# Attention scores from two float32r parts, matmuls paired in two 64-row tiles, value matmuls half a stretch later

## What is computed

```python
# per sequence
h = _layernorm(x) * (1 + ca) + sa
q, k, v = lora_linear(h, wq, aq, bq), lora_linear(h, wk, ak, bk), lora_linear(h, wv, av, bv)   # 16 heads of 16
scores = jnp.einsum('bhqd,bhkd->bhqk', q, k) / jnp.sqrt(16.)
attn = jax.nn.softmax(jnp.where(causal, scores, -jnp.inf))
x = x + ga * lora_linear(jnp.einsum('bhqk,bhkd->bhqd', attn, v), wo, ao, bo)
h = _layernorm(x) * (1 + cb) + sb
x = x + gb * ffn(h)          # relu(h Wi^T + expert low rank), top 2 of 4 experts, then Wo
```

## Time and profile before

| what | value |
|---|---|
| three runs | 2151.85, 2151.95 and 2155.94 us, median 2151.95 us |
| span of the profiled execution (first to last instruction) | 2145.5 us |
| own time of the profiled execution | not on the page; the span is 6.4 us below the median of the runs |
| mean granted TensorE clock | 0.959 of full |
| TensorE matmul records, busy | 88% of the span |
| TensorE weight loads, busy | 46% |
| DVE, ACT, POOL busy | 56%, 44%, 25% |
| one turn of the loop | 251.1 us (its reload of the input at 320.0 and at 1575.4 us, five turns apart) |

### The profile page before, as it was taken

The page is one execution under the profiler, slowest core; times in us unless marked ns, Lnnn a source line. Parts: engine busy times, 40 slices in busy tenths (PEclk is TensorE's granted clock), DMA queues, the critical chain, the costliest instruction groups (busy, mean ns, idle before and its releaser), DMA issues.

```text
span 2145.5 us, 36829 instructions
## 1 busy us (share of the span) xinstructions
PE 1892.0 (88%) x11124; PEld 980.5 (46%) x11124; DVE 1199.8 (56%) x2697; ACT 938.8 (44%) x1701; POOL 529.7 (25%) x823
## 2 busy tenths in 40 slices
PE   8687888999889989899889998899898998798858
PEld 5233343455435454354534555354543545344435
DVE  3755567555665557655575556655576554755132
ACT  2254444544444544544444444444445443544421
POOL 3111122322222212223223222222122232132223
PEclk9889989999999999999999999999999999999979
DMA  5523333121433222232331214332222323210100
GB/s 170 80 50 60 60 57 78 22 63 23 80 60 67 33 39 77 31 70 32 65 79 20 62 24 81 60 67 33 36 70 41 70 31 65 31 26 16 35 0 20
DMA packets 72349, 111.82 MB, mean 52 GB/s; under 512 B 13940, under 2 KB 41680, under 8 KB 72152
## 3 DMA queue, kind: packets, MB, share of 16 engines
q1 hardware_dynamic: 72136, 109.31, 27.3%
q10 hardware_dynamic: 16, 0.02, 0.0%
HBM read 75.20 MB, written 33.57 MB: 51 GB/s over the span
## 4 chain that ended last, share of the span: by engine, by line
PE 61%; DVE 14%; DMA 8%; issue 7%; SPq 5%; ACT 4%; POOL 0%; DVEq 0%; POOLq 0%; ACTq 0%
PE mxs L747 11%; PE ov L776 9%; PE st L761 9%; PE dense L856 8%; DMA k_st<-k_parts_scratch 8%; PE dense L841 5%; DVE negm L1147 4%; PE dense L867 4%; PE dense L791 4%; SPq L577 4%; PE dense L833 3%; PE dense L733 3%; PE mxs L751 2%; SPq L581 1%; DVE stats L1018 1%
## 5 line engine op out<-in xcount | busy, mean ns | idle before, releaser
L915 ACT ACTIVATE probs<-st 128x512 f32<-128x512 f32 (+1 forms) x1216 | 666.9, 576 | 651.2 <-PE st L761 613.2
L747 PE MATMUL mxs<-k_st,q_st 96*128 96x512 bf16 (+3 forms) x1536 | 463.4, 333 | 54.6 <-DMA k_st<-k_parts_scratch 48.2
L1147 DVE TENSOR_REDUCE negm<-mxs 128x1 f32<-128x512 f32 (+4 forms) x736 | 416.1, 613 | 147.8 <-PE mxs L751 147.4
L761 PE MATMUL st<-q_st,k_st 98*128 98x512 bf16 (+3 forms) x1536 | 453.0, 335 | 38.9 <-issue 24.3
L1147 DVE TENSOR_REDUCE negm_left<-mxs 128x1 f32<-128x512 f32 x512 | 330.0, 684 | 168.0 <-PE mxs L747 165.5
L776 PE MATMUL ov<-probs,v_g 128*32 128x512 f32 (+3 forms) x3072 | 333.5, 506 | 22.7 <-POOL probs L634 21.9
L747 PEld LDWEIGHTS mxs<-k_st,q_st 96*128 96x128 bf16 x1536 | 149.0, 98 | 333.9 <-issue 101.7
L856 PE MATMUL dense<-c_t,wi_t 128*128 128x512 f32 x512 | 247.3, 605 | 4.3 <-ACT ratio_b L965 3.7
L631 POOL TENSOR_TENSOR fence<-fence 128x1 f32<-128x1 f32 x256 | 49.9, 195 | 756.8 <-ACT probs L915 756.6
L761 PEld LDWEIGHTS st<-q_st,k_st 98*128 98x128 bf16 x1536 | 140.1, 99 | 202.6 <-issue 76.3
L655 POOL TENSOR_TENSOR hid<-hid,second 128x512 f32<-128x512 f32 x128 | 159.8, 1270 | 245.1 <-DVE second L1211 244.6
(11 more groups left out here) (162 smaller groups left out, 1715.3 us busy)
## 6 DMA issues: line engine op xcount, KB each, us to landing
q_st<-q_parts_scratch SPq DMA_DIRECT2D x192, 128.0 KB, 6.9
k_st<-k_parts_scratch SPq DMA_DIRECT2D x192, 128.0 KB, 7.4
q_parts_scratch<-q_part SPq DMA_DIRECT2D x16, 768.0 KB, 3.3
k_parts_scratch<-k_part SPq DMA_DIRECT2D x16, 768.0 KB, 5.4
xin<-in_L_attn_x SPq DMA_DIRECT2D x9, 1024.0 KB, 5.1
x<-in_L_attn_x SPq DMA_DIRECT2D x8, 1024.0 KB, 10.6
out_x<-ob SPq DMA_DIRECT2D x64, 128.0 KB, 1.7
q_st<-m_row SPq DMA_DIRECT2D x128, 4.0 KB
```

What stands on the lines that cost most here:

```text
L747: last = nc.tensor.matmul(mxs[:, bank_m, j * n:(j + 1) * n], q_st[0:KS, slot, h0 + j, qt * P:(qt + 1) * P], k_st[0:KS, slot, h0 + j, k0:k0 ...
L761: last = nc.tensor.matmul(st[:, score_bank(ch, kt, h0), j * n:(j + 1) * n], k_st[0:KS + 2, slot, h0 + j, kt * P:(kt + 1) * P], q_st[0:KS + ...
L915: nc.scalar.activation(probs[:, par, h0:h0 + heads, 0:n], st[:, score_bank(ch, kt, h0), 0:heads * n].rearrange("p (j q) -> p j q", q=n), A ...
L1147: nc.vector.tensor_reduce(dst[:, h0:h0 + heads], src, axis=AX.X, op=ALU.max, negate=True).then_inc(max_free, 1)
```

## The change

The planner and its consumers are changed together:

- q and k are split into two float32r parts instead of three bfloat16 ones: ACT writes part 0, DVE one subtraction for part 1; the second DVE operation and POOL's are gone. `q_part` and `k_part` hold one half of the heads at a time, not two.
- Three products of parts make 48 rows (50 with the maximum). Two heads share the array: one on partitions 0 to 63, one on 64 to 127, each as a 64-row tile with its own PSUM bank.
- `mx` works on two banks at a time, one per tile, and waits for all but the last bank of the step before. There are 42 banks, 21 steps, for a group. The mask is one matmul per bank.
- `qk` fills both banks of `st`, for one pair of heads (two pairs where the unit has at most 256 queries), waits for the exp of the step before, and ACT makes one exp over both banks. A group has 20 such steps and exps.
- `pv` of a unit stands in the middle of the next stretch; `probs` has three buffers. `ce` moves one unit later.
- Score steps are placed beside the nearest `mx` step. The planner's costs and `row_maxima` are new.
- The ones of `k_st` are loaded by eight small DMAs at the start.

```diff
+    banks += [(h, heads, qt, qt // 4) for h in range(HG // heads)]
+def max_steps():
+    banks = max_banks()
+    return [(i, banks[i], banks[i + 1]) for i in range(0, len(banks), 2)]
...
-    return [("qk", slot, c, kt, h, heads) for h in range(0, HG, heads)]
+    pairs = 2 if unit_queries(c, kt)[1] <= 256 else 1
+    return [("qk", slot, c, kt, p, pairs) for p in range(0, HG // 2, pairs)]
...
-        return (max_keys(qt, chunk) + P * (qt // 4 == chunk)) * heads / 2.4
+        return 200 + (max(max_keys(qt, chunk), 256) + 2 * P * (qt // 4 == chunk)) * heads / 2.4
...
-    row_maxima = [0, 3, 4, 4, 5, 5, 6, 6, 6, 0, 0, 0] if post else [0, 4, 4, 5, 6, 6, 5, 5, 4, 0, 0, 0]
+    unit_cost = [500 + (2 * max(n, 256) + 4 * n) / 2.4 for n in (unit_queries(c, kt)[1] for c, kt in UNITS)]
+    row_maxima = [0, 2, 2, 2, 3, 3, 3, 3, 3, 0, 0, 0] if post else [0, 2, 2, 3, 3, 3, 3, 3, 2, 0, 0, 0]
...
-        turns += [((i + 0.35) / len(mx), 1, s) for i, s in enumerate(mx)]
+        pairs_at = [(i + 0.5) / len(mx) for i in range(len(mx))]
+        turns = [(at, 1, s) for at, s in zip(pairs_at, mx)]
+        for i, s in enumerate(following):
+            at = (i + 0.5) / len(following)
+            turns.append((min(pairs_at, key=lambda t: abs(t - at)) if mx else at, 0, s))
+        if u or post:
+            turns.append((0.5, 3, ("pv", (u - 1) // NU % 2, *UNITS[k - 1])))
...
-        q_part = sb("q_part", [P, 2, 3, S], BF16)
-        q_st = sb("q_st", [P, 2, HG, S], BF16)
-        probs = sb("probs", [P, 2, HG, HB])
+        q_part = sb("q_part", [P, 2, S], F32R)
+        q_st = sb("q_st", [P, 2, HG // 2, S], F32R)
+        probs = sb("probs", [P, PROBS, HG, HB])
...
+                    after(pe, max_free, 2 * done("mx") - MAX_BANKS + 2)
+                    for j in range(heads):
+                        for i in range(2):
+                            rows = slice(HALF * i, HALF * i + SK)
+                            last = nc.tensor.matmul(mxs[:, (first + i) % MAX_BANKS, j * n:(j + 1) * n],
+                                                    q_st[rows, slot, banks[i][0] // 2 + j, qt * P:(qt + 1) * P],
+                                                    k_st[rows, slot, banks[i][0] // 2 + j, k0:k0 + n], ...)
...
-                    after(pe, exp_done, done("qk") - SCORE_BANKS + 1)
+                    after(pe, exp_done, done("qk"))
+                    for p in range(pairs):
+                        for i in range(2):
+                            rows = slice(HALF * i, HALF * i + SK + 2)
+                            last = nc.tensor.matmul(st[:, i, p * n:(p + 1) * n],
+                                                    k_st[rows, slot, p0 + p, kt * P:(kt + 1) * P],
+                                                    q_st[rows, slot, p0 + p, q0:q0 + n], start=True, stop=True)
...
+                    heads = probs[:, par, 2 * p0:2 * (p0 + pairs), 0:n].rearrange("p (j b) q -> p b j q", b=2)
+                    nc.scalar.activation(heads, st[:, :, 0:pairs * n].rearrange("p b (j q) -> p b j q", q=n),
...
-                    after(dve, part3_ready, done("pj") - 1)
-                    nc.vector.tensor_tensor(rest[:, par, :], db[:, :], dst[:, 0, :],
+                    nc.vector.tensor_tensor(dst[:, 1, :], db[:, :], dst[:, 0, :].bitcast(F32),
-                    nc.vector.tensor_copy(dst[:, 1, :], rest[:, par, :]).then_inc(part2_ready, 1)
```

More of the change, by code:

```diff
@@ L26 @@
 F32 = mybir.dt.float32
+F32R = mybir.dt.float32r
 BF16 = mybir.dt.bfloat16
@@ L121, in body_plan @@
     if post:
-        put(0, *[("ct", i) for i in range(4)])
+        put(1, ("ce", GROUPS - 1, 1), *[("ct", i) for i in range(4)])
     if pre:
@@ L125, in body_plan @@
     if post:
-        put(1, *[("op", i) for i in range(4)])
+        put(2, *[("op", i) for i in range(4)])
     if pre:
@@ L228, in prologue_plan @@
     for i, s in enumerate(beside):
[L229 to L230 removed]
+        plan += [s] + mx[3 * i:3 * i + 3]
+    assert 3 * len(beside) >= len(mx)
     plan += [("ms",), ("ps", 1), ("nm", 0)] + score_steps(0, *UNITS[0])
@@ L545, in _ @@
             sp.dma_start(bg_b[:, :], bg.partition_broadcast(P)).then_inc(ffn_in, 16)
+            sp.wait_ge(ones_ready, 1)
+            for half in range(2):
+                for slot in range(2):
+                    for p in range(HG // 2):
+                        sp.dma_start(k_st[HALF * half + SK:HALF * half + SK + 2, slot, p, :].bitcast(F32),
+                                     ones).then_inc(ones_in, 16)
             def run(step, done, it, bank):
@@ L559, in run @@
                     ot = a[0]
-                    stacked = [held(sp, done(f"rs{s}") * (2 * SPLIT * 16)) for s in range(2)]
-                    split = held(sp, done("pj"))
-                    sp.wait_ge(part3_ready, split)
+                    stacked = [held(sp, done(f"rs{s}") * (STACK_DMAS * 16)) for s in range(2)]
+                    split = [held(sp, done(f"bank{i}")) for i in range(2)]
+                    for i in range(2):
+                        after(sp, dense_free[i], split[i])
                     for s in range(2):
@@ L753, in run @@
-                    last.then_inc(max_full, 1)
+                        for i in range(2):
+                            rows = slice(HALF * i, HALF * i + SK)
+                            last = nc.tensor.matmul(mxs[:, (first + i) % MAX_BANKS, j * n:(j + 1) * n],
+                                                    q_st[rows, slot, banks[i][0] // 2 + j, qt * P:(qt + 1) * P],
+                                                    k_st[rows, slot, banks[i][0] // 2 + j, k0:k0 + n],
+                                                    start=(j == 0), stop=True, skip_group_check=True)
+                            if not diagonal:
+                                last.then_inc(max_full, 1)
@@ L754, in run @@
+                    if diagonal:
+                        for i in range(2):
+                            tri = mxs[:, (first + i) % MAX_BANKS, 0:heads * n].rearrange("p (j k) -> p j k", k=n)
+                            nc.tensor.matmul(tri[:, :, n - P:n], ident_b[:, :],
+                                             causal_b[:, :].unsqueeze(1).broadcast_to([P, heads, P]),
+                                             start=False, stop=True, skip_group_check=True).then_inc(max_full, 1)
                 elif kind == "qk":
-                    slot, ch, kt, h0, heads = a
+                    slot, ch, kt, p0, pairs = a
@@ L756, in run @@
                     q0, n = unit_queries(ch, kt)
-                    if (ch, kt, h0) == (*UNITS[0], 0):
+                    if (ch, kt, p0) == (*UNITS[0], 0):
                         pe.wait_ge(m_row_in, done("nm") * (HG * 16))
-                    after(pe, exp_done, done("qk") - SCORE_BANKS + 1)
-                    for j in range(heads):
-                        last = nc.tensor.matmul(st[:, score_bank(ch, kt, h0), j * n:(j + 1) * n],
-                                                k_st[0:KS + 2, slot, h0 + j, kt * P:(kt + 1) * P],
-                                                q_st[0:KS + 2, slot, h0 + j, q0:q0 + n], start=True, stop=True)
+                    after(pe, exp_done, done("qk"))
@@ L947, in run @@
                     which, ot, half = a
-                    dst = (q_part if which == "q" else k_part)[:, ot, :, half * HB:(half + 1) * HB]
+                    dst = (q_part if which == "q" else k_part)[:, :, half * HB:(half + 1) * HB]
                     if isinstance(it, int) and it < 0:
                         act.wait_ge(gates_out, 16)
-                    after(act, parts_out[ot], done(f"ps{ot}") * (2 * 16))
+                    for stored in range(2):
+                        after(act, parts_out[stored], done(f"ps{stored}") * (2 * 16))
                     nc.scalar.copy(dst[:, 0, :], db[:, :]).then_inc(part1_ready, 1)
```

167 lines of the change are left out of this document (72 added, 95 removed).

## The result

The changed kernel takes 2676.91 us (median of four runs), the kernel before 2152.48 us: a ratio of 1.2436, 95% interval 1.2413 to 1.2459. It is slower by a quarter, far outside the predicted range.

What follows compares the result with a forecast made beforehand. TensorE's instruction stream was taken as the bound; 2145.5 - 240 + 237 - 42 + 28 = 2128.5 us of span, plus 6.4 and some 1 us of prologue, gave 2136 us. Own range 2085 to 2160, whole range 2040 to 2275 us.

Steps and rivals of the forecast that it cites:

- Score and maximum matmuls: TensorE's `qk` and `mx` matmuls: two heads at once take 266 us in all instead of 506, saving 240 us.
- Changes of tile shape: TensorE entering and leaving 64-row tiles: 325 us in 32 groups, before 88 us, a cost of 237 us.
- Waits that go: TensorE's waits for POOL's triangle, the copy of `ov` and the stacked parts shrink, a gain of 42 us.
- hidden by a group of stretches in the body: The DMAs of `ps` send a third more bytes, hidden in the body; 3 us may show in the prologue.
- Waits that come: TensorE's new waits: 22 us for exps ahead of `qk`, 6 us more for maxima and queued relus; cost 28 us.
- The slower rival, the single exp buffer: In units 4 to 8 score steps find the exp still running; 2186 to 2216 us, chance 0.20.
- +50 at five steps: Smaller case of the single exp buffer: five of 20 score steps a group wait, adding 50 us to the forecast.
- The list of signs: What the trace would show if right or wrong; wrong included a granted clock below 0.96.
- Cheaper tile changes: Rival: entries to and exits from 64-row tiles cost 80 to 118 us less, 2018 to 2056 us; chance 0.15.
- loads in a row: Rival: the two tiles' float32r weight loads cannot run together, costing 144 us, 2280 us; chance 0.17.
- no pairing: Rival: pairs run one after the other or float32r takes a float32 record's time; 2400 us, chance 0.06.

Runs made afterwards that it cites:

- b_rows48: On the kernel before, score and maximum matmuls read 48 and 50 rows instead of 96 and 98; 2575.29 us, ratio 1.1972.
- a_bf16: On the changed kernel, bfloat16 in place of float32r for the two parts; 2455.56 us, ratio 1.1414.
- b_tight: On the kernel before, score steps wait for the exp of the step before, maximum steps for all banks but one; 2465.54 us, ratio 1.1465.
- a_short: On the changed kernel, exps and maxima work on a quarter of the columns; 2330.88 us, ratio 1.0861.

## Why the prediction was wrong, point by point

- **Score and maximum matmuls** (saving 240): right. The two matmuls of a pair start 0.003 us apart, in one pass, 0.22 us for 512 columns, as priced; the two loads run side by side.
- **Changes of tile shape** (cost 237): not contradicted as a price of stream. The rest of the balance fell by 41 us, where the sum had 3, and it can be off by twice that. I counted 800 entries into 64-row tiles; counted along the trace there are 730. The change was priced at full clock. In `b_rows48` the clock took 240 us beside the 236 of the changes; how much of the 240 the changes bring, and how much the 48 rows, is open.
- **Waits that go** (gain 42): POOL's went. That the moved value step is a gain is a step with the wrong sign: the move cost 226 us on the changed kernel. The prediction asked what the value step waits for and not what waits behind it: at the end of its stretch it had covered exps, `m_w` and the load. The wait for the parts, said to fall by 10 us, rose by 40; with half the bytes, in `a_bf16`, it is 17.2 us. And the step "hidden by a group of stretches in the body" failed for the halved `q_part`: ACT waited 48.4 us, six times up to 8.1 us, for the store of the parts before the next projection could be written, and TensorE 28.7 us behind it.
- **Waits that come** (cost 28): mis-sized tenfold, and with the clock this is the step that failed most. I took two places a group at 0.35 us, 64 places in all; there were 216 of 0.67 us for exps, and 123 us for maxima. The 1.5 us from a score step to free banks was nearly right: 0.50 for the matmuls, 0.04 and 1.04 for the exp. What was wrong is how often two score steps stand closer than that once the value step has left the boundary: where TensorE waited for an exp it was ready 0.94 us after the start of the last score step in the median. ACT's other work, as at 1351.34, adds some 15 us. The slower rival, the single exp buffer, named the right mechanism and priced it at 102 us without the clock (its +50 at five steps should read +42). Some 100 of the 144.6 us stand where it put them, before the score steps issued in units 4 to 8, and 35 us in units 0 and 1. `b_tight` shows the two bonds at 315 us in a kernel with no other change.
- **The clock**, not a step at all: no term stood for it. The list of signs named a clock under 0.96 as what would make the prediction wrong, yet no rival used it. It is 283 us, of a miss of 541. `b_tight` and `a_short` tie it to the waits in part (0.928 by waits alone, back to 0.909 with most of them gone), and the places fit: from the score steps of unit 6 to those of unit 7 the lower level was granted 70% of the time, before 0%. The part that goes with rows and changes of tile is not separated.
- **Cheaper tile changes, loads in a row, no pairing**: none happened. The Trainium skill (TensorEngine Tiling, Key Properties) was right that a change of mode drains the array, and the runs agree at 0.09 us a change. Its rule of loads that overlap only across row groups (TensorE: Matmul & The Clock Gate, The mechanism), read strictly, is not what the trace shows: the loads of the second pair in a run, at 1345.16, start 0.11 us behind the first pair's and under its stream (the timeline of TensorE's weight loads):

```profile
1345.05 0.19 PEld L760 LDWEIGHTS st<-q_st,k_st 50*128 50x128 f32 x2 [0.16 <-issue]
1345.16 0.19 PEld L739 LDWEIGHTS mxs<-k_st,q_st 48*128 48x128 f32 x2
```

The same section of the Trainium skill, ahead of that rule, also lets a load go ahead of matmuls in flight when it goes to the background weight buffer, and these two rows fit that.

## What to carry to other kernels

Price a change of a TensorE-bound kernel twice: what it adds to the stream, and what it may do to the clock, which multiplies the work of the whole kernel: it fell here with more waits, and with fewer rows and the changes of tile that 48 of them bring. Slack that looks generous may be needed: taking one bank from each of two rings cost 15% here with not one instruction changed. And work moved away from the end of a stretch may have been the cover of someone's latency: ask of every step that moves what waits behind it, test such a move by itself, and look in the trace whether the test moved what it was meant to move.

## What was not expected of the hardware

- A matmul of 48 or 50 rows ran, by all signs, in a 64-row tile by its row count alone, and paid 0.10 us at each meeting with a full-array one; 65 rows did not.
- TensorE's clock, of the two levels 1.2 and 2.4 GHz, was at the lower one for some 900 of 2670 us in the changed kernel and 175 of 2145 us before, though no single wait was longer than 12.2 us and of the changed kernel's 561 waits 474 were below 1 us.
- Two thirds of the rows in the same instructions lowered the mean granted clock, from 0.950 to 0.956 in eleven executions to 0.935 to 0.945 in five.
- Relieving one of two bonds gave 78 or 136 us, both 346 us.
